# Choosing the experts with bf16 one-hot arrays whose innermost index is the token tile, with fewer small operations around them

## The reference

```
logits = jnp.einsum('tc,ec->te', x_flat, router_w)
probs = jax.nn.softmax(logits, axis=-1)
top_w, top_idx = jax.lax.top_k(probs, K)
...
sel = jnp.take_along_axis(y, top_idx[:, :, None], axis=1)
out = jnp.einsum('tkc,tk->tc', sel, top_w)
```

## Time and profile before

| | us |
|---|---|
| median of 3 runs (lowest, highest) | 724.86 (723.36, 732.24) |
| profiled execution, its time | 723.68 |
| its span | 721.9 |
| DVE busy in it | 520.4 |
| PE busy | 514.8 |
| POOL busy | 439.5 |
| ACT busy | 327.4 |

### The profile page before, as it was taken

One profiled execution on the slowest core, in us unless ns is written; L12 is line 12 of the kernel. 1 busy time (PEld: TensorE's weight loads), 2 busy tenths in 40 slices (PEclk: granted clock), 3 DMA queues, 4 the chain that ended last, 5 costly groups with the idle time before them and its releaser, 6 DMA issues.

```text
span 721.9 us, 8687 instructions
## 1 busy us (share of the span) xinstructions
PE 514.8 (71%) x1884; PEld 274.2 (38%) x1885; DVE 520.4 (72%) x1002; ACT 327.4 (45%) x629; POOL 439.5 (61%) x335
## 2 busy tenths in 40 slices
PE   4567979979998889507999990677118777377740
PEld 2223334434433333405777770245113222055530
DVE  5938899897999899295434335358884889867747
ACT  3265854763774454111333344746014656691005
POOL 0039899998898989115777765217126666057750
PEclk9877999998998799756999996888557999779995
DMA  5043456433332420093111224001001115301125
GB/s 181 1 155 126 146 160 209 153 102 105 103 117 88 142 91 15 15 393 138 52 52 51 49 50 124 0 0 30 29 4 45 47 39 38 119 34 51 47 70 148
DMA packets 36658, 63.52 MB, mean 88 GB/s; under 512 B 5202, under 2 KB 22164, under 8 KB 36116
## 3 DMA queue, kind: packets, MB, share of 16 engines
q1 hardware_dynamic: 30996, 51.64, 21.8%
q0 software_dynamic: 5632, 11.55, 6.7%
HBM read 53.99 MB, written 9.18 MB: 88 GB/s over the span
## 4 chain that ended last, share of the span: by engine, by line
PE 49%; DVE 24%; issue 9%; ACT 7%; DMA 4%; POOL 3%; DVEq 2%; SPq 0%; POOLq 0%; ACTq 0%
PE ps L969 12%; PE ps L1083 9%; PE ps L1068 5%; DVE hs L1515 5%; PE ps L936 4%; PE ps L963 3%; PE ps L1075 2%; PE ps L1152 2%; DVE p_hot L1406 2%; PE ps L1218 2%; DVEq L1586 2%; DVE ys L1753 1%; DVE prod L1525 1%; POOL bu L450 1%; DMA down_s<-in_down 1%
## 5 line engine op out<-in xcount | busy, mean ns | idle before, releaser
L450 POOL TENSOR_TENSOR bu<-uT,b_sb 128x1024 f32<-128x1024 f32 x64 | 151.0, 2381 | 29.4 <-DVE uT L1495 29.4
L969 PE MATMUL ps<-prod,cst 128*128 128x512 f32 x256 | 129.5, 653 | 3.0 <-DVE yT L1535 2.9
L416 POOL DMA_INDIRECT y_dram<-ys,rows_i x88 | 86.9, 987 | 54.6 <-DVE ys L1753 35.8
L410 POOL DMA_INDIRECT xl<-h_dram,rows_i x88 | 88.1, 1001 | 47.6 <-PE ps L1062 18.1
L624 ACT ACTIVATE ps<-dtT,neg_a 128x512 f32<-128x512 f32 x128 | 85.4, 684 | 50.5 <-DVE hs L1515 49.9
L461 POOL TENSOR_TENSOR prod<-hs,c_sb 128x1024 f32<-128x1024 f32 x32 | 76.2, 2380 | 16.1 <-PE ps L969 13.0
L969 PEld LDWEIGHTS ps<-prod,cst 128*128 128x128 f32 x256 | 50.1, 206 | 82.0 <-issue 76.4
L1515 DVE TENSOR_TENSOR_SCAN hs<-ps,bu 128x512 f32<-128x512 f32 x64 | 73.7, 1203 | 9.7 <-ACT ps L624 9.6
L1515 DVE TENSOR_TENSOR_SCAN hs<-ps,carry,bu 128x512 f32<-128x512 f32 x64 | 77.6, 1263 | 3.4 <-ACT ps L624 3.1
L1218 PE MATMUL ps<-mf_s,xt 128*128 x96 | 55.5, 665 | 16.8 <-ACT xt L707 11.9
L1591 DVE TENSOR_TENSOR hp<-ps,b_s 128x512 f32<-128x512 f32 x40 | 27.7, 692 | 34.7 <-PE ps L1068 34.7
(11 more groups left out here) (246 smaller groups left out, 930.7 us busy)
## 6 DMA issues: line engine op xcount, KB each, us to landing
b_sb<-b_rows SPq DMA_DIRECT2D x32, 512.0 KB, 4.6
c_sb<-b_rows SPq DMA_DIRECT2D x32, 256.0 KB, 3.7
w_s<-in_w SPq DMA_DIRECT2D x17, 256.0 KB, 4.0
mf_s<-in_mf SPq DMA_DIRECT2D x1, 4096.0 KB, 17.0
h_dram<-h_tok SPq DMA_DIRECT2D x8, 256.0 KB
b_s<-in_b SPq DMA_DIRECT2D x1, 2048.0 KB, 7.8
phase_s<-in_phase SPq DMA_DIRECT2D x1, 2048.0 KB, 21.4
down_s<-in_down SPq DMA_DIRECT2D x1, 2048.0 KB, 8.0
```

The source lines that it names most:

```text
L410: pool.indirect_dma_start(xl[:, j % XR, :], None, h_dram[l], bass.IndirectOffsetOnAxis(ap=rows_i[:, 0, j:j + 1], axis=0)).then_inc(loaded[ ...
L416: pool.indirect_dma_start(y_dram[l], bass.IndirectOffsetOnAxis(ap=rows_i[:, 1, j:j + 1], axis=0), ys[:, j % XR, :], None).then_inc(saved[j ...
L450: nc.gpsimd.tensor_tensor(bu[:, g % RING, :, :], uT[:, c % 2, :, :], b_sb[:, k % BRING, g % 2, :].unsqueeze(1).broadcast_to([P, ND, CHUNK] ...
L969: last = nc.tensor.matmul(bank(Y_BANK + d), ident, prod[:, g % RING, d, :], start=n == 0, stop=n == NS - 1)
```

## The change

- `p_hot`, `j_rows` and `j_hot` get the token tile as innermost index, so that PE reads them with a step of 16 elements of 2 bytes. What they are compared with, `p_rep` and `j_rep`, is written out once in bf16 (`scales`), and `tile_of` and `row_of` are bf16.
- `pick` has fewer small operations: both ranks are handled together, copies are left out, `xcmp` to `tile_i` come after `rows_i`.
- `p_next` and `spare` (4 small instructions, before in each `pick`) are made once, on DVE between `uT` and the first scan. `scales` stands beside the last projection in layer 0 and before the first logits in layer 1.
- The last projection goes to PSUM bank FRONT. `gate_y` comes before the copy of the logits, and `best_two` of the first 12 token tiles before the last logits.
- In the last pair of a chunk PE adds product 13 before it waits for product 14.

```diff
--- before.py
+++ after.py
@@ -228,15 +232,16 @@
-        p_hot, e = place("p_hot", [P, PICKS, P], BF16, at=y0_at)
-        j_rows, e = place("j_rows", [P, PICKS, 2 * ST1], BF16, at=e)
-        j_hot, e = place("j_hot", [P, PICKS, ST1], BF16, at=e)
+        p_hot, e = place("p_hot", [P, 2, P, NTILE], BF16, at=y0_at)
+        j_rows, e = place("j_rows", [P, 2, 2 * ST1, NTILE], BF16, at=e)
+        j_hot, e = place("j_hot", [P, 2, ST1, NTILE], BF16, at=e)
+        p_rep, e = place("p_rep", [P, P, NTILE], BF16, at=e)
+        j_rep, e = place("j_rep", [P, ST1, NTILE], BF16, at=e)
-        tile_of, e = place("tile_of", [P, 2, NTILE], at=e)
-        row_of, e = place("row_of", [P, 2, NTILE], at=e)
+        slot_m, e = place("slot_m", [P, 2, NTILE], at=e)
+        tile_of, e = place("tile_of", [P, 2, NTILE], BF16, at=e)
+        row_of, e = place("row_of", [P, 2, NTILE], BF16, at=e)
-        p_next, e = place("p_next", [P, 1], at=e)
-        spare, e = place("spare", [P, ST1], at=e)
@@ -272,7 +277,7 @@
             c, n = divmod(g, NS)
-            return c * NS + (1 if n == 0 else NS if n == NS - 1 else n if n % 2 == 0 else n + 2)
+            return c * NS + (1 if n == 0 else n + 1 if n >= NS - 3 else n if n % 2 == 0 else n + 2)
         def conv_bank(c, d):
@@ -282,6 +287,9 @@
             return (FRONT, BACK)[d]
+
+        def out_bank(c):
+            return BACK if c + 1 < NCHUNK else FRONT
         def z_bank(c, d):
@@ -421,13 +429,15 @@
                     pool.wait_ge(S["j_hot_ready"], 2 * l + k + 1)
-                    nc.gpsimd.tensor_tensor(j_rows[:, ks, 0:st], j_hot[:, ks, 0:st],
-                                            cst[:, K["jiota"]][:, ks].unsqueeze(2).broadcast_to([P, NTILE, st]),
+                    nc.gpsimd.tensor_tensor(j_rows[:, k, 0:st, :], j_hot[:, k, 0:st, :],
+                                            cst[:, K["jiota"]][:, ks].unsqueeze(1).broadcast_to([P, st, NTILE]),
                                             ALU.mult).then_inc(S["hi_ready"], 1)
...
@@ -903,8 +912,9 @@
                     pe.wait_ge(S["p_hot_ready"], 2 * l + k + 1)
-                    for g in range(k * NTILE, (k + 1) * NTILE):
-                        last = nc.tensor.matmul(ps[:, 3, 0:2 * st], p_hot[:, g, :], j_rows[:, g, 0:2 * st], start=g == 0, stop=g == PICKS - 1)
+                    for t in range(NTILE):
+                        last = nc.tensor.matmul(ps[:, 3, 0:2 * st], p_hot[:, k, :, t], j_rows[:, k, 0:2 * st, t],
+                                                start=k + t == 0, stop=k == 1 and t == NTILE - 1)
                 last.then_inc(S["table_ps"], 1)
@@ -977,12 +987,12 @@
                     pe.wait_ge(S["dt_ready"], 2 * c + 4)
-                if c:
+                if c and c + 1 < NCHUNK:
                     pe.wait_ge(S["logit_sb"], c)
                     for d in range(ND):
-                        last = nc.tensor.matmul(ps[:, BACK, t * P:(t + 1) * P], yT[:, d, t * P:(t + 1) * P],
+                        last = nc.tensor.matmul(ps[:, out_bank(c), t * P:(t + 1) * P], yT[:, d, t * P:(t + 1) * P],
                                                 wout_g[:, c // 2, d, :], start=d == 0, stop=d == ND - 1)
@@ -990,6 +1000,8 @@
                     pe.wait_ge(S["dt_ready"], 2 * c + 6)
+                if c + 1 == NCHUNK:
+                    pe.wait_ge(S["logit_sb"], c)
                 for t in range(CT):
@@ -1024,13 +1036,16 @@
                     after[m](c - 1)
+                if m == NS // 2 - 1:
+                    pe.wait_ge(S["prod_pool"], k)
+                    add_up(2 * k - 1)
                 pe.wait_ge(S["prod_ready"], k + 1)
                 add_up(2 * k)
-                if m:
+                if 0 < m < NS // 2 - 1:
                     pe.wait_ge(S["prod_pool"], k)
@@ -1352,6 +1367,15 @@
                         then(nc.vector.scalar_tensor_tensor(out=et(3), in0=et(1), scalar=LOWEST, in1=et(0), op0=ALU.mult, op1=ALU.add))
+            def scales(st):
+
+                j3 = cst[:, K["jiota"]]
+                p8 = p_iota[:, :].rearrange("p (a b) -> p a b", b=E1)
+                then(nc.vector.scalar_tensor_tensor(out=p8, in0=j3[:, 0:P // E1].unsqueeze(2).broadcast_to([P, P // E1, E1]), scalar=-float(E1),
+                                                    in1=cst[:, K["eiota"]].unsqueeze(1).broadcast_to([P, P // E1, E1]), op0=ALU.mult, op1=ALU.subtract))
+                then(nc.vector.tensor_copy(p_rep[:, :, :], p_iota[:, :].unsqueeze(2).broadcast_to([P, P, NTILE])))
+                then(nc.vector.tensor_scalar(j_rep[:, 0:st, :], j3[:, 0:st].unsqueeze(2).broadcast_to([P, st, NTILE]), float(P), None, ALU.mult))
+
             def pick(l, e_n, st):
@@ -1371,47 +1395,27 @@
                     nc.vector.tensor_tensor(route[:, 8, 0:NTILE], m12[:, 1, :], m12[:, 0, :], ALU.subtract).then_inc(S["pick_exp"], 1)
...
                 dve.wait_ge(S["rank_ps"], l + 1)
...
+                then(nc.vector.tensor_tensor_scan(route[:, 5, 0:n], cst[:, K["reset"]][:, 0:n], ps[:, 2, 0:n], 0.0, ALU.mult, ALU.add))
                 tot = route[:, 5, 0:n].rearrange("p (e t) -> p e t", t=NTILE)[:, :, NTILE - 1]
...
+                then(nc.vector.tensor_scalar(tiles_e[:, 0, 1:e_n + 1], tot, P / 2 - 0.5, MAGIC_P, ALU.add, ALU.add))
+                then(nc.vector.tensor_tensor_scan(tiles_e[:, 1, 0:e_n + 1], minus_m[:, 0:e_n + 1], tiles_e[:, 0, 0:e_n + 1], 0.0, ALU.add, ALU.add))
+                then(nc.vector.tensor_tensor(route[:, 5, 0:n], route[:, 5, 0:n], ps[:, 1, 0:n], ALU.subtract))
+                then(nc.vector.tensor_tensor(et(5), et(5), tiles_e[:, 1, 0:e_n].unsqueeze(2).broadcast_to([P, e_n, NTILE]), ALU.add))
+                two = route[:, 6:8, 0:n]
+                then(nc.vector.tensor_tensor(two, route[:, 1:3, 0:n], route[:, 5, 0:n].unsqueeze(1).broadcast_to([P, 2, n]), ALU.mult))
+                nc.vector.tensor_reduce(slot_f[:, 0, :], te(6), axis=AX, op=ALU.add)
+                then(nc.vector.tensor_reduce(slot_f[:, 1, :], te(7), axis=AX, op=ALU.add))
+                then(nc.vector.tensor_scalar(slot_m[:, :, :], slot_f[:, :, :], 0.5 - P / 2, MAGIC_P, ALU.add, ALU.add))
+                nc.vector.tensor_scalar(tile_of[:, :, :], slot_m[:, :, :], MAGIC_P, None, ALU.subtract)
+                then(nc.vector.scalar_tensor_tensor(out=row_of[:, :, :], in0=slot_m[:, :, :], scalar=-MAGIC_P, in1=slot_f[:, :, :],
+                                                    op0=ALU.add, op1=ALU.subtract))
                 for k in range(2):
...
+                    nc.vector.tensor_tensor(j_hot[:, k, 0:st, :], j_rep[:, 0:st, :], tile_of[:, k, :].unsqueeze(1).broadcast_to([P, st, NTILE]),
                                             ALU.is_equal).then_inc(S["j_hot_ready"], 1)
...
+                for k in range(2):
+                    nc.vector.tensor_tensor(p_hot[:, k, :, :], p_rep[:, :, :], row_of[:, k, :].unsqueeze(1).broadcast_to([P, P, NTILE]),
+                                            ALU.is_equal).then_inc(S["p_hot_ready"], 1)
                 dve.wait_ge(S["table_ps"], l + 1)
@@ -1420,10 +1424,16 @@
                                                     op0=ALU.is_equal, op1=ALU.mult))
...
+                nc.vector.tensor_tensor(rows_i[:, 0, 0:st], rows_f[:, 0, 0:st], picked[:, 0:st], ALU.add)
+                nc.vector.scalar_tensor_tensor(out=rows_i[:, 1, 0:st], in0=picked[:, 0:st], scalar=-1.0, in1=rows_f[:, 1, 0:st],
+                                               op0=ALU.add, op1=ALU.add).then_inc(S["rows_ready"], 1)
+                cmp = xcmp[TAB:TAB + 1, 0:st * e_n].rearrange("p (j e) -> p j e", e=e_n)
+                then(nc.vector.scalar_tensor_tensor(out=cmp, in0=cst[TAB:TAB + 1, K["jiota"]][:, 0:st].unsqueeze(2).broadcast_to([1, st, e_n]),
+                                                    scalar=float(P), in1=tiles_e[TAB:TAB + 1, 1, 1:e_n + 1].unsqueeze(1).broadcast_to([1, st, e_n]),
+                                                    op0=ALU.mult, op1=ALU.is_ge))
+                then(nc.vector.tensor_reduce(tile_f[TAB:TAB + 1, 0:st], cmp, axis=AX, op=ALU.add))
+                then(nc.vector.tensor_scalar(tile_f[TAB:TAB + 1, 0:st], tile_f[TAB:TAB + 1, 0:st], float(e_n - 1), None, ALU.min))
+                nc.vector.tensor_copy(tile_i[TAB:TAB + 1, l, 0:st], tile_f[TAB:TAB + 1, 0:st]).then_inc(S["tiles_ready"], 1)
                 dve.wait_ge(S["tiles_ready"], l + 1)
@@ -1538,7 +1547,7 @@
                 xs = x_tok[:, c * CT:(c + 1) * CT, :]
-                nc.vector.tensor_tensor(xs, xs, bank(BACK).rearrange("p (t c) -> p t c", c=C), ALU.add).then_inc(S["x_added"], 1)
+                nc.vector.tensor_tensor(xs, xs, bank(out_bank(c)).rearrange("p (t c) -> p t c", c=C), ALU.add).then_inc(S["x_added"], 1)
                 dve.wait_ge(S["x_added"], c + 1)
@@ -1548,6 +1557,10 @@
             dt_and_u(0, 1)
+            then(nc.vector.tensor_reduce(p_next[:, :], cst[:, K["tri"]], axis=AX, op=ALU.add))
```

(10 more changed lines are left out.)

52 lines of the change are left out of this document (9 added, 43 removed).

## The result

| | before | changed |
|---|---|---|
| median, us (20 runs each) | 726.02 | 717.23 |
| lowest, highest | 723.3, 733.89 | 713.92, 729.88 |

The ratio is 0.9873 with a 95% interval of 0.9836 to 0.9910: 9 us faster, a little over one per cent, so inside the 2% that the prediction called "within". Two later groups of runs gave the same kernel 0.9908 (0.9866 to 0.9949) and 0.9915 (0.9877 to 0.9952), 6.7 and 7.0 us between the medians.

A forecast was written before the change was run, and what follows sets the result against it. Bound: mostly PE and DVE, with a serial DVE thread from `mask_b` to each layer's first gather. Terms -2.9 + 0 + 2.4 + 1.1 + 4.6 - 1.5 - 2.6 + 5.5 = +6.6 took 723.68 to 717.1 us, range 706 to 724.

The forecast's parts named there:

- within: Whole kernel: measured time no more than about 2% (14.5 us) from no change, given 84%.
- Small instructions: Before the first scan: TENSOR_SCALARs held behind POOL's `bu` start the scan late, -2.9 us (0 to -2.9).
- Additions: Scan, last products of a chunk: same matmuls in another order, 0 us (-1 to +1).
- Gate and projection: End of layer 0's scan: earlier `gate_y` shortens PE's idle time, projection stays at full clock, +2.4 us.
- best_two: Before `mask_b` in layer 0: twelve tiles' worth moves into DVE's idle time, +1.1 us (+0.5 to +1.5).
- Choice in layer 0: `mask_b` to first gather: 13.75 us against 18.35, with DVE at half rate and dearer strided matmuls, +4.6 us.
- The strided rival: Table matmuls: PE pays for the step, 735.3 us at 0.44 each, no gain from 0.26; slower than before 9%.
- Gathers and bulk: Layer 0's first gather, issued earlier, shares the DMA engines with the bulk loads, -1.5 us.
- a first gather that lands more than 6 us after its issue: Layer 0's first gather: listed among what the profile would show if the prediction was wrong.
- the gather waits for the bulk: Layer 0's first gather: waits for the end of the bulk, 4.4 us more than counted, 721.5 us, 12%.
- scales in layer 1: Between router and choice in layer 1: `scales` has no cover on DVE, -2.6 us (-2.2 to -4.2).
- Choice in layer 8: Layer 1, `mask_b` to first gather: 16.1 us against 21.59, +5.5 us.

The follow-up runs named there:

- the four edits together: Changed kernel with bulk loads in four pieces, `scales` once, `j_rows` on DVE, four small instructions ahead of `uT`: median 708.61 us, 0.9795 of the kernel before.

## Why the prediction was right, and where it was not

The forecast time and its mechanism held: a serial DVE thread in each layer, shortened by 4.5 and 4.8 us where 4.6 and 5.5 were written. By its own steps:

1. **Small instructions, -2.9: failed.** The step "I take 2.9, since the earlier trace rows shows a held TENSOR_SCALAR and no row shows a free one". The single-element one is free, and the earlier trace rows names what the step left out: the scan waited for ACT's decay until 4.44 us after the first `bu` began, nearly as long as two held ones take. 4.72 against 4.44 us, and 4.44 again when they are moved (the four edits together): -0.3.
2. **Additions, 0: no sign against it.** The medians of the two orders are 0.1 us apart, and the shortest scan stages with the new order, 239.5 to 239.8 us, stand beside 240.2 before. An effect of 2 us would not have been seen.
3. **Gate and projection, +2.4: right**, +2.46. That it hangs on PE's idle time is shown by the run with `gate_y` back behind the copy.
4. **best_two, +1.1:** +1.4.
5. **Choice in layer 0, +4.6:** +4.5. Half rate and serial POOL were both right, the last matmuls were priced at 2.45 us and DVE waited 2.91 for them. I had put the price of the step on "the last 16"; in fact PE never catches up, since the first 16 take 2.5 us as well and end when the second `p_hot` does. The strided rival was to decide from 0.26 us a matmul; it came to 0.16. What the Trainium skill says of lines of 16 bytes (SBUF - State Buffer, Door 1: The DMA port swizzle) agrees with the 0.159 us for the moving operand, and not with the weights, whose step cost nothing more (0.079 us with `j_rows` alone compact). The half rate itself mattered less than its price suggests: with the full price but matmuls at 0.077 us the choice was only 1.0 us longer here and 0.6 in layer 1.
6. **Gathers and bulk, -1.5: mis-sized.** 4.2 us in the profile, 3.4 to 3.9 in the repeats. The step "between nothing and waiting for the end I take -1.5" underrated how long a small gather waits beside another queue: its first packet began 4.4 us after its issue, where it is 1.9 without the bulk, and its packets then took turns with larger ones. A sign of being wrong, "a first gather that lands more than 6 us after its issue", did come. In ten executions with the bulk in its old place the first matmul came 31.2 to 32.7 us after the addition of the projection, while the gather was issued from 24.4 (`j_rows` on DVE) to 26.9 us (`j_rows` without a step) after it: of 2.4 us by which the choice was faster, 1.5 reached the matmul. Before the change it was 34.1, with the gather at 31.4. The rival "the gather waits for the bulk" had the right direction, but not the mechanism: it counted 5.9 us for a wait to the end, and the gather lost 4.2 and landed before that end.
7. **scales in layer 1, -2.6:** -2.44, and given back when `scales` is called once.
8. **Choice in layer 1, +5.5:** +4.8. POOL's two `j_rows` took 4.49 us together beside `p_hot`, which ended 11.75 us after `mask_b` (11.7 written), but the matmuls were 0.187 us each, 5.99 for 32, and finished 3.6 us behind it where I had 2 x 1.48 = 2.96.

Steps 1 and 6 miss by +2.6 and -2.7 and cancel. So the total is closer than its parts deserve; without this luck it would have been 2.6 us off to either side. There is luck in the starting point as well. The 6.6 us were taken from one execution of 723.68; taken from the median of 726.02 they give 719.4, and the measured gain was 8.8 us, with 6.7 and 7.0 in the later groups.
